# A four-layer graph network on one core: the key sums of the first layer turned, and 1,200 instead of 1,100 edge chunks counted densely

## The chip, the core and the metric

The kernel runs on one NeuronCore of a Trainium2 chip. The core's engines are TensorE (PE in the rows; PEld is its weight load), VectorE (DVE), ScalarE (ACT), GpSimd (POOL) and SyncE (SP, which here only issues DMAs). Each runs its own instruction stream, and they meet at semaphores. The metric is device time in microseconds of one execution; lower is better. SBUF is the on-chip memory of 128 partitions, PSUM holds what TensorE writes, and DRAM tables are reached by DMA.

## The reference

```python
# x (12500, 64); src, dst (400000,), dst sorted; edge_type (400000,) 0 or 1; two edge weights
head = x[src]; rel = relation_emb[edge_type]
score = sigmoid(concat([head, rel]) @ att_w + att_b)
aggr = segment_sum(score * x[dst], src)                 # first layer: sums by src
x = layernorm(x + tanh(aggr @ W0.T + b0))
agg = segment_sum(x[src], dst); deg = segment_sum(1, dst)   # second layer: sums by dst
x = layernorm(x + where(deg > 0, agg, x) @ W1.T + b1)
x = layernorm(x + segment_sum(x[src] * w1, dst))        # third
x = layernorm(x + segment_sum(x[src] * (w2 * w1), dst)) # fourth
```

In the first layer the score depends on the source node and the edge type alone. So the kernel needs, for each pair (node, type), which it calls a key (`2 * src + type`), the plain sum of `x[dst]` over the edges with that key. It multiplies by the score afterwards.

## The kernel before

The 400,000 edges, sorted by `dst`, are 3,125 chunks of 128. A group is 5 chunks (`GC`). Since `dst` is sorted, and denser at low numbers, a chunk of low number touches only 3 to 6 neighbouring nodes (`rows_of`).

**The first layer's main stage** forms the key sums in two ways at once.

*By table*, for the groups from `G00 = C0 // GC` on, `NT0 = 405` of them (`for n in range(NT0)`). DVE (`keys0`) compares each chunk's keys with each other. PE gathers (L1036) and multiplies with `x` (L1053), so that every first edge of a key holds the chunk's whole message for it. ACT copies the message into one of two buffers (`MSGS = 2`, L872) once the scatters that read that buffer have landed. POOL then issues five indirect DMAs that add the 128 messages of each chunk into one of three DRAM tables (L718).

*Densely*, for the first `C0 = 1100` chunks. They are cut into 800 blocks of 1 to 5 chunks. DVE makes a one-hot array for a block (`block_hots0`, L1410), ACT the other factor ("codes", L825 and L830), and PE multiplies the two (`block_sums0`, L1002): this counts how many edges of each key go to each of the block's few nodes. DVE adds the counts into a window of 64 nodes (`block_add0`, L1435). Blocks are listed in windows (`SEGS0`), 29 of them. When the blocks of a window are in, the window is emptied in 25 units (`NU`) of up to 4 tiles of 128: PE turns the counts (`turn`, L1014), ACT copies them to SBUF and clears the window (L844, L849), PE multiplies by the window's rows of `x` (`key_sums`, L1025), and DVE adds the product to `acc` (`key_add`, L1450). There is one set of window counts, so the blocks of the next window start only when all 25 units are through. `xb`, the window's rows of `x`, stands as a block-diagonal 128 x 128: x for type 0 in one corner, x for type 1 in the other.

**The order** is written out ahead by `slots()`: it spreads the dense work over the table groups by costs per block (`0.13*k*d + 0.24*d`) and per unit (2.4). Every engine runs group n of the table work together with the blocks and units of slot n. Before, a slot is worth 7.74 of these cost units.

**The end of the first layer** goes in `NB = 14` batches of 7 node tiles. SP loads a batch of the three tables (L615), POOL adds the three together (L769, L771), DVE adds `acc` (L1528), multiplies by the scores (L1532) and adds the two types (L1536). PE transposes (`turn_sums`, L1074) and multiplies by W0 (`times_w0`, L1082), ACT copies (L883) and takes the tanh (L889), and DVE does the layernorm (L1541 to L1566). Three more layers follow, of other code: the change does not touch them.

Of the kernel before, what the change touches and what calls it, by code (L numbers as in the profile page):

```python
# [17 lines left out]
F32, I32, I16, BF16 = mybir.dt.float32, mybir.dt.int32, mybir.dt.int16, mybir.dt.bfloat16  # L18
# [4 lines left out]
P = 128  # L23
# [8 lines left out]
T = (N + P - 1) // P  # L32
NP = T * P
LAST = N - (T - 1) * P
BT_ = 7
NB = T // BT_
BN = BT_ * P
KEYS = 2 * NP
ROWS = KEYS + P
# [6 lines left out]
NT = (C - CD) // GC  # L46
# [11 lines left out]
BR = 10  # L58
PSD = 4
FZ = 14  # L60
C0 = 1100
G00 = C0 // GC
NT0 = NG - G00
MSGS = 2
# [42 lines left out]
NSEG = len(SEGS) - 1  # L107
SEGS0, SEG_OF0 = segments(NB0, WD, 5)
NS0 = len(SEGS0) - 1
# [67 lines left out]
NU = -(-T // 4)  # L177
# [10 lines left out]
def padded(n):  # L188
    return -(-n // 8) * 8


ND, ND0, NTT = padded(NBLK), padded(NB0), padded(NT)


NCB = CD - C0
# [25 lines left out]
def program(nc, x, src, dst, edge_type_2, edge_weight, edge_weight_n2, rel, att_w, att_b, W0, b0, W1, b1, out):  # L221
    ctx = ExitStack()
    with ctx:
        def sb(name, shape, dt=F32):
            return ctx.enter_context(nc.sbuf_tensor(name, shape, dt))

        def sem(name):
            return ctx.enter_context(nc.semaphore(name))
# [19 lines left out]
        src_i = src_i.bitcast(I32)  # L248
        y = big[:, 0:2 * CQ * P]
        w1_c, w12_c = (big[:, 2 * CQ * P + k * C:2 * CQ * P + (k + 1) * C] for k in range(2))  # L250
        dinfo = sb("dinfo", [1, ND + ND0 + NTT + 64 + 32 + padded(NCB)], I16)

        xs = sb("xs", [P, T * XW])
        acc = sb("acc", [P, NP])


        arena = mem[:, 0:AR]
# [88 lines left out]
        bmin, segb, boff = (arena[0:1, 3125 + k * ND:3125 + k * ND + NBLK] for k in range(3))  # L346
        rows0 = 3125 + 3 * ND
        segb0, boff0 = (arena[0:1, rows0 + k * ND0:rows0 + k * ND0 + NB0] for k in range(2))
        gmin = arena[0:1, rows0 + 2 * ND0:rows0 + 2 * ND0 + NT]
        rows1 = rows0 + 2 * ND0 + NTT  # L350
        sbase, sbase0 = arena[0:1, rows1:rows1 + NSEG], arena[0:1, rows1 + 32:rows1 + 32 + NS0]
        nq_row = stat[0:1, 0:Q]
        assert NSEG <= 32 and NS0 <= 32 and rows1 + 32 + NS0 <= 8455
        STAGED = AR + 2 * CQ * P + 2 * NTAB * BN


        offs_i, offs0_i, cols_i, bases_i, bases0_i, cbase_i = (
            dinfo[:, sum(m[:k]):sum(m[:k + 1])] for m in [(ND, ND0, NTT, 64, 32, padded(NCB))] for k in range(6))
        si = y[:, 0:CD].bitcast(I32)
        badr = r_src  # L360
        kd = dst_l[:, 0:CD]
# [12 lines left out]
        BK = 512  # L374
# [11 lines left out]
        iota_p = ps[:, 7 * BK:7 * BK + DT // 2].bitcast(I16)  # L386
        ps_T = [ps[0:F + 1, 4 * p * BK:4 * p * BK + BN] for p in range(2)]
        ps_B = ps_O = [ps[:, (2 + p) * BK:(2 + p) * BK + BT_ * F] for p in range(2)]
        ps_wt = ps[0:F, 6 * BK:6 * BK + 2 * F]
        ps_dg = ps[:, 6 * BK:6 * BK + T]  # L390

# [20 lines left out]
        z_done, zt_ps = ([sem(f"{n}{l}") for l in range(2)] for n in ("z_done", "zt_ps"))  # L412
        zt_sb, b_done, own_add, deg_ps = (sem(n) for n in ("zt_sb", "b_done", "own_add", "deg_ps"))
        tab_sum, th_done, y_done = sem("tab_sum"), sem("th_done"), sem("y_done")
        tb_in = [sem(f"tb_in{p}") for p in range(2)]
        cmin_done, row_w, row_l, base_done, rows_done = (sem(n) for n in (
            "cmin_done", "row_w", "row_l", "base_done", "rows_done"))
# [549 lines left out]
        def _(pe):  # L967
# [49 lines left out]
            def key_sums(u):  # L1017
                s_, i = u // NU, u % NU
                pe.wait_ge(at_done, u + 1)
                if i == 0:  # L1020
                    pe.wait_ge(xb_in[s_ % 2], (s_ // 2 + 1) * 32)
                if u >= 2:
                    pe.wait_ge(s_add, u - 1)
                for k in range(min(4, T - 4 * i)):
                    last = pe.matmul(ps_s[u % 2][:, k * P:(k + 1) * P], at_sb[u % 2][:, k * P:(k + 1) * P], xb[s_ % 2],  # L1025
                                     start=True, stop=True)
                last.then_inc(s_sum, 1)

            for n in range(NT0):
                kw = rows_of((G00 + n) * GC)  # L1030
# [38 lines left out]
            def turn_sums(b):  # L1069
                pe.wait_ge(z_done[0], b + 1)  # L1070
                if b >= 2:
                    pe.wait_ge(zt_sb, b - 1)
                for k in range(BT_):
                    last = pe.transpose(ps_T[b % 2][0:F, k * P:(k + 1) * P], zb[b % 2][:, k * F:(k + 1) * F], ident[:, :])  # L1074
                last.then_inc(zt_ps[0], 1)

            def times_w0(b):
# [5 lines left out]
                                     start=True, stop=True)  # L1083
                last.then_inc(b_done, 1)

            for b in range(NB + 1):
                if b < NB:
                    turn_sums(b)
                if b:
                    times_w0(b - 1)  # L1090
# [120 lines left out]
        def _(dve):  # L1211
# [312 lines left out]
            def table_sum(b):  # L1524
                v.wait_ge(tab_sum, 2 * (b + 1))
                if b:
                    v.wait_ge(z_done[0], b)
                v.tensor_tensor(tsum, stage[b % 2][:, 0:BN], acc[:, b * BN:(b + 1) * BN], ALU.add).then_inc(sum_done, 1)  # L1528
                v.wait_ge(sum_done, b + 1)
                t4 = tsum.rearrange("p (j t f) -> p j t f", t=2, f=F)  # L1530
                a4 = att.rearrange("p (t j) -> p j t", t=2)[:, b * BT_:(b + 1) * BT_, :]
                v.tensor_tensor(t4, t4, a4.unsqueeze(3).to_broadcast([P, BT_, 2, F]), ALU.mult).then_inc(e0x, 1)  # L1532
                v.wait_ge(e0x, b + 1)
                if b >= 2:
                    v.wait_ge(zt_ps[0], b - 1)
                v.tensor_tensor(zb[b % 2].rearrange("p (j f) -> p j f", f=F), t4[:, :, 0, :], t4[:, :, 1, :],  # L1536
                                ALU.add).then_inc(z_done[0], 1)
# [273 lines left out]
```

## Time and profile before

| | |
|---|---|
| median of 3 runs | 11974.94 us (11965.58 to 11983.21) |
| profiled execution | 11986.64 us |
| its span, first to last instruction | 11984.9 us |
| POOL, DVE, PE, ACT busy, share of the span | 68%, 63%, 73%, 47% |
| first scatter of the first layer | 103.5 us from the start |
| last scatter | 3888.0 us |
| first gather of the second layer | 4044.92 us |

The profile shows one execution. Times in its rows are microseconds from the start of the span; "busy" is time in which an engine works, and the brackets give idle time ahead of an instruction and what ended it. L718 is line 718 of the kernel. A matmul's printed duration includes its latency, so that back-to-back matmuls overlap in the rows; a merged row's second number is the time from the first start to the last end. One f32 matmul of the code stands as two MATMUL instructions, a transpose as one.

### The profile page before, as it was taken

The page shows a single profiled execution, that of the slowest core. Times are in us where ns is not written, and L with a number is a line of the kernel's source. Part 1 is how long each engine was busy: PE and PEld are TensorE (multiplying, and loading weights), DVE is VectorE, ACT ScalarE, POOL GpSimd, SP SyncE. Part 2 cuts the span into 40 slices and gives each one's busy share as a digit, 9 for nine tenths or more (in the row PEclk, how much of TensorE's full clock was granted, in tenths as well). Part 3 has the DMA queues.
Part 4 walks back from the last instruction along what each step waited for, and adds up shares of the span by engine and source line. Part 5 has one row for each costly group of instructions (what it writes and reads, how often), then busy time and mean ns, then how long its engine had stood idle before and what let it go on. Part 6 is the DMA issues. An engine that isn't in the chain of part 4 may idle for free. (4 is left out here: it accounts for less than half of the span.)

```text
span 11984.9 us, 177157 instructions
## 1 busy us (share of the span) xinstructions
PE 8764.2 (73%) x52953; PEld 6104.8 (51%) x52954; DVE 7520.0 (63%) x19055; ACT 5637.8 (47%) x12807; POOL 8164.1 (68%) x7269
## 2 busy tenths in 40 slices
PE   4777777777776455666666788878887788888886
PEld 2555556565564334445445545545445355444455
DVE  7676666666664655544443777666665776666665
ACT  4655554444443344333332566544443665544443
POOL 5888888888888666666666466666666566666665
PEclk7777777777776576777777799999889899889898
DMA  5343334434433311111111111111111111111111
GB/s 145 38 48 38 39 38 39 38 38 39 38 39 38 87 25 25 24 24 25 24 24 24 29 24 25 25 25 24 25 24 26 30 24 25 25 25 25 23 24 29
DMA packets 669272, 405.76 MB, mean 34 GB/s; under 512 B 471754, under 2 KB 581068, under 8 KB 667065
## 3 DMA queue, kind: packets, MB, share of 16 engines
q0 software_dynamic: 460320, 255.76, 17.8%
q1 hardware_dynamic: 204196, 135.29, 4.4%
q8 instruction: 443, 7.26, 0.3%
q10 hardware_dynamic: 3814, 3.37, 0.1%
q14 instruction: 499, 4.09, 0.1%
HBM read 286.44 MB, written 107.44 MB: 33 GB/s over the span
## 5 line engine op out<-in xcount | busy, mean ns | idle before, releaser
L797 POOL DMA_INDIRECT mem<-xt,mem x5175 | 4897.7, 946 | 2886.3 <-issue 1337.2
L1132 PE MATMUL ps<-mem 128*128 128x392 f32 (+5 forms) x6750 | 2914.1, 537 | 1051.8 <-DVE mem L1688 432.1
L718 POOL DMA_INDIRECT table<-mem,idx x2025 | 3149.6, 1555 | 710.3 <-issue 600.8
L1688 DVE TENSOR_TENSOR mem<-mem,ps 128x392 f32 (+3 forms) x3300 | 1917.1, 581 | 1971.6 <-remote 1002.4
L939 ACT ACTIVATE mem<-iota_f,mem 128x128 f32<-128x128 f32 x4200 | 1319.3, 390 | 2635.6 <-remote 1281.9
L1144 PE MATMUL ps<-mem,xs 128*64 128x94 f32 (+1 forms) x17640 | 2064.1, 270 | 387.2 <-issue 370.2
L1144 PEld LDWEIGHTS ps<-mem,xs 128*64 128x64 f32 (+1 forms) x17640 | 1792.1, 155 | 1045.7 <-issue 994.6
L1669 DVE TENSOR_SCALAR mem<-ps,mem 128x392 f32<-128x392 int16 (+5 forms) x4050 | 2175.1, 556 | 0.0
L1132 PEld LDWEIGHTS ps<-mem 128*128 128x128 f32 (+1 forms) x6750 | 1108.5, 185 | 1910.5 <-issue 1303.2
L918 ACT COPY mem<-zero_c 128x658 f32<-128x658 f32 x1260 | 895.8, 732 | 1403.1 <-remote 966.4
L1165 PE MATMUL ps<-mem 128*64 128x64 f32 (+1 forms) x10350 | 1024.4, 243 | 505.5 <-issue 477.3
L1165 PEld LDWEIGHTS ps<-mem 128*64 128x64 f32 (+1 forms) x10350 | 865.1, 155 | 922.1 <-issue 892.5
L1025 PE MATMUL ps<-mem 128*128 128x128 f32 x5684 | 885.5, 313 | 345.8 <-ACT mem L844 325.7
L1002 PE MATMUL ps<-mem 128*128 128x392 bf16 (+2 forms) x2200 | 712.8, 462 | 472.0 <-DVE mem L1435 381.3
L1025 PEld LDWEIGHTS ps<-mem 128*128 128x128 f32 x5684 | 816.0, 223 | 401.6 <-ACT mem L844 370.0
L1450 DVE TENSOR_TENSOR acc<-acc,ps 128x512 f32<-128x512 f32 (+1 forms) x700 | 472.5, 677 | 807.8 <-PE ps L1025 702.4
L1435 DVE TENSOR_TENSOR mem<-mem,ps 128x784 f32 (+2 forms) x800 | 785.3, 982 | 195.0 <-PE ps L1002 85.4
L950 ACT ACTIVATE mem<-mem 128x128 f32<-128x128 f32 x2800 | 879.9, 390 | 18.4
L1703 DVE TENSOR_TENSOR acc<-acc,ps 64x64 f32 (+1 forms) x1035 | 217.1, 210 | 1034.0 <-remote 805.6
L872 ACT COPY mem<-ps 128x320 f32<-128x320 f32 x405 | 172.3, 425 | 1322.2 <-DMA table<-mem,idx 1011.2
L1053 PE MATMUL ps<-mem 64*128 64x64 f32 (+2 forms) x4050 | 713.8, 336 | 82.7 <-ACT mem L857 82.6
L1053 PEld LDWEIGHTS ps<-mem 64*128 64x128 f32 (+2 forms) x4050 | 649.6, 244 | 217.2 <-issue 100.0
(178 smaller groups left out, 7691.6 us busy)
## 6 DMA issues: line engine op xcount, KB each, us to landing
mem<-xt,mem POOLq DMA_INDIRECT x5175
mem<-key_rows SPq DMA_DIRECT2D x405, 160.0 KB
table<-mem,idx POOLq DMA_INDIRECT x2025
table<-mem POOLq DMA_DIRECT2D x3, 6304.0 KB
mem<-table SPq DMA_DIRECT2D x42, 448.0 KB, 5.3
xt<-xs SPq DMA_DIRECT2D x9, 896.0 KB
mem<-in_x_dram SPq DMA_DIRECT2D x403, 16.0 KB
mem<-in_x_dram SPq DMA_DIRECT2D x250, 1.2 KB
```

Source lines behind the costliest of these rows:

```text
L718: pool.indirect_dma_start(out=tables[i % NTAB][:, :], out_offset=bass.IndirectOffsetOnAxis(ap=idx[:, i % (IDXS * GC):i % (IDXS * GC) + 1], ...
L797: pool.indirect_dma_start(out=gbuf[:, o:o + F], out_offset=None, in_=xt[l][:, :], in_offset=bass.IndirectOffsetOnAxis(ap=src_q[q % 2].bitc ...
L918: act.copy(dense[zi // FZ % 2][:, lo * WC:hi * WC], zero_c[:, :].to_broadcast([P, (hi - lo) * WC])).then_inc(cleared[l], 1)
L939: ins = act.activation(lo_d[:, k * P:(k + 1) * P], iota_f[:, 0:P], ACT.Abs, bias=nslo_q[q % 2][:, c + k:c + k + 1])
L950: ins = act.mul(lo_l[:, o + k * P:o + (k + 1) * P], lo_d[:, k * P:(k + 1) * P], wd_q[q % 2][:, c + k:c + k + 1])
L1025: last = pe.matmul(ps_s[u % 2][:, k * P:(k + 1) * P], at_sb[u % 2][:, k * P:(k + 1) * P], xb[s_ % 2], start=True, stop=True)
L1053: last = pe.matmul(ps_m[:, k * F:(k + 1) * F], bts[0:kw, k * P:(k + 1) * P], rhs, start=True, stop=True)
L1132: last = pe.matmul(ps_d[b % PSD][:, 0:w], lo_l[:, r * P:(r + 1) * P], blk_l[:, r * DT:r * DT + w], start=(k == 0), stop=(k == parts - 1))
L1144: last = pe.matmul(ps_f[0:M, :], xs[:, t * XW:t * XW + M], dense[s_ % 2][:, t * WC:(t + 1) * WC], start=(t == 0), stop=(t == T - 1), skip_ ...
L1165: last = pe.matmul(ps_w[n % 2][0:M, :], gbuf[:, o:o + M], ohr[:, q:q + WD], start=(k == 0), stop=(k == GC - 1), skip_group_check=True)
L1669: ins = v.tensor_scalar(blk_l[:, r * DT:r * DT + w], iota_p[:, 0:w], kd_q[q % 2][:, at + k:at + k + 1], None, ALU.is_equal)
L1688: v.tensor_tensor(at, at, new, ALU.add).then_inc(d_add[l], 1)
```

## The change

**Key sums.** The counts, which were the weights of four f32 matmuls of 128 columns, are now streamed as up to 512 columns through one f32 matmul whose weights are the block-diagonal `xb`. Its result is transposed: `acc` holds (type, feature) on the partitions and nodes along the free dimension. So each of the 98 tiles of `acc` must be turned back before the tables are added to it. `turn_back` does this on PE in two parts for each batch, 4 tiles and 3 tiles, through one PSUM bank, and DVE adds the tables in two pieces from there.

**Dense chunks.** `C0` goes from 1100 to 1200. Then `NT0` is 385 instead of 405, there are 900 blocks instead of 800 (the 100 new ones of one chunk and 5 rows each), 35 windows instead of 29, 875 units instead of 725, and 1,925 scatters instead of 2,025. `slots()` spreads the greater dense work over fewer table groups: a slot is worth 9.62 cost units. The rest of the diff finds room for the longer lists.

```diff
+BACK = [(0, 4), (4, BT_)]
-C0 = 1100
+C0 = 1200
...
+        ps_back = ps[:, 6 * BK:7 * BK]
...
         # key_sums
-                for k in range(min(4, T - 4 * i)):
-                    last = pe.matmul(ps_s[u % 2][:, k * P:(k + 1) * P], at_sb[u % 2][:, k * P:(k + 1) * P], xb[s_ % 2],
-                                     start=True, stop=True)
-                last.then_inc(s_sum, 1)
+                w = min(4, T - 4 * i) * P
+                pe.matmul(ps_s[u % 2][:, 0:w], xb[s_ % 2], at_sb[u % 2][:, 0:w], start=True, stop=True).then_inc(s_sum, 1)
...
+            def turn_back(b, half):
+                if b or half:
+                    pe.wait_ge(back_used, 2 * b + half)
+                lo, hi = BACK[half]
+                for k in range(lo, hi):
+                    t = b * BT_ + k
+                    last = pe.transpose(ps_back[:, (k - lo) * P:(k - lo + 1) * P], acc[:, t * P:(t + 1) * P], ident[:, :])
+                last.then_inc(back_ps, 1)
+
+            pe.wait_ge(s_add, NU * NS0)
+            turn_back(0, 0)
             for b in range(NB + 1):
                 if b < NB:
+                    turn_back(b, 1)
+                    if b + 1 < NB:
+                        turn_back(b + 1, 0)
                     turn_sums(b)
                 if b:
                     times_w0(b - 1)
...
         # table_sum
-                v.tensor_tensor(tsum, stage[b % 2][:, 0:BN], acc[:, b * BN:(b + 1) * BN], ALU.add).then_inc(sum_done, 1)
-                v.wait_ge(sum_done, b + 1)
+                for half, (lo, hi) in enumerate(BACK):
+                    v.wait_ge(back_ps, 2 * b + half + 1)
+                    v.tensor_tensor(tsum[:, lo * P:hi * P], stage[b % 2][:, lo * P:hi * P], ps_back[:, 0:(hi - lo) * P],
+                                    ALU.add).then_inc(back_used, 1)
+                v.wait_ge(back_used, 2 * (b + 1))
+                v.sem_inc(sum_done, 1)
```

The order on PE in the stretch where the blocks have three rows (128x294): L1002 is `block_sums0`, L1053 and L1036 the table group's two steps. Before:

```order
L1002 MATMUL ps<-mem 128x294 x14
L1053 MATMUL ps<-mem 128x64 x5
L1036 MATMUL ps<-mem 64x128 x5
L1002 MATMUL ps<-mem 128x294 x12
L1053 MATMUL ps<-mem 128x64 x5
```

and after the change, where these lines are L1006, L1055 and L1038:

```order
L1006 MATMUL ps<-mem 128x294 x16
L1055 MATMUL ps<-mem 128x64 x5
L1038 MATMUL ps<-mem 64x128 x5
L1006 MATMUL ps<-mem 128x294 x18
L1055 MATMUL ps<-mem 128x64 x5
```

A block is two of these matmuls, so 7 blocks stood beside one table group, and 8 or 9 stand there now.

The order on PE while a window is emptied: L1014 are the transposes, L1025 the key sums, 4 and 4 to a unit. Before:

```order
L1053 MATMUL ps<-mem 128x64 x5
L1036 MATMUL ps<-mem 64x128 x5
L1014 MATMUL ps<-ident,mem 128x128 x8
L1025 MATMUL ps<-mem 128x128 x4
L1014 MATMUL ps<-ident,mem 128x128 x4
L1025 MATMUL ps<-mem 128x128 x8
L1053 MATMUL ps<-mem 128x64 x5
```

and after, with L1018 and L1029 for the same:

```order
L1055 MATMUL ps<-mem 128x64 x5
L1038 MATMUL ps<-mem 64x128 x5
L1018 MATMUL ps<-ident,mem 128x128 x8
L1029 MATMUL ps<-mem 128x512
L1018 MATMUL ps<-ident,mem 128x128 x4
L1029 MATMUL ps<-mem 128x512
L1018 MATMUL ps<-ident,mem 128x128 x4
L1029 MATMUL ps<-mem 128x512 x2
L1055 MATMUL ps<-mem 128x64 x5
```

Three units stood between two table groups, and four stand there now; a unit's four products are one.

The order on PE at the end of the layer, where L1074 turns a batch's sums and L1082 multiplies them by W0. Before:

```order
L1074 MATMUL ps<-ident,mem 64x128 x14
L1082 MATMUL ps<-w0T,mem 128x64 x7
L1074 MATMUL ps<-ident,mem 64x128 x7
L1082 MATMUL ps<-w0T,mem 128x64 x7
L1074 MATMUL ps<-ident,mem 64x128 x7
```

and after, where L1094 is `turn_back`, L1076 and L1084 the other two:

```order
L1094 MATMUL ps<-ident,acc 128x128 x11
L1076 MATMUL ps<-ident,mem 64x128 x7
L1094 MATMUL ps<-ident,acc 128x128 x7
L1076 MATMUL ps<-ident,mem 64x128 x7
L1084 MATMUL ps<-w0T,mem 128x64 x7
L1094 MATMUL ps<-ident,acc 128x128 x7
```

The 3 tiles of a batch's second part now stand behind the W0 product of the batch two before it, and 4 tiles of the next batch's first part follow them.

## Rows read from the trace of the kernel before

**Rows 1.** Windows: start:end and length, busy (instructions) by engine, clock, DMA.
```profile
200.00:3800.00 3600.00, 2764.36 (x16446) 2104.51 (x16444) 2374.06 (x7652) 1854.06 (x3502) 3001.24 (x1939) 0.74 0.40 39
1237.00:1265.00 28.00, 26.72 (x229) 24.88 (x228) 18.06 (x65) 16.92 (x33) 23.42 (x16) 1.00 0.39 38
1194.00:1237.00 43.00, 32.86 (x150) 21.50 (x150) 35.82 (x113) 23.53 (x42) 34.44 (x23) 0.53 0.41 39
1237.00:1302.00 65.00, 50.18 (x383) 43.99 (x381) 36.60 (x126) 34.44 (x69) 54.32 (x36) 0.88 0.40 39
3902.00:4038.00 136.00, 64.26 (x294) 58.35 (x294) 109.11 (x105) 34.81 (x53) 85.31 (x43) 0.50 0.55 142
```

**Rows 2.** Waits from 1000 to 3800: who waited for whom, in total, times, longest.
```profile
ACT mem L872 <- DMA table<-mem,idx: 695.6, 164, 9.4
...
PE ps L1002 <- DVE mem L1435: 327.4, 334, 6.0
...
DVE mem L1435 <- PE ps L1002: 58.8, 72, 1.4
...
POOL table L718 <- ACT mem L872: 4.4, 5, 2.1
```

**Rows 3.** Timeline, POOL: start, us, instruction, idle before it.
```profile
1302.48 1.54 POOL L718 DMA_INDIRECT table<-mem,idx  x1 [0.30 <-issue]
```

**Rows 4.** Timeline, ACT's message copies, 1207 to 1296, and POOL where it stood.
```profile
1207.30 0.43 ACT L872 COPY mem<-ps 128x320 f32<-128x320 f32 x1 [4.08 <-DMA table<-mem,idx]
1218.39 0.43 ACT L872 COPY mem<-ps 128x320 f32<-128x320 f32 x1
...
1219.10 1.54 POOL L718 DMA_INDIRECT table<-mem,idx  x1 [2.10 <-ACT mem L872]
...
1231.53 0.43 ACT L872 COPY mem<-ps 128x320 f32<-128x320 f32 x1 [2.48 <-PE ps L1053]
1242.98 0.43 ACT L872 COPY mem<-ps 128x320 f32<-128x320 f32 x1 [1.99 <-PE ps L1053]
1250.67 0.43 ACT L872 COPY mem<-ps 128x320 f32<-128x320 f32 x1 [1.99 <-PE ps L1053]
...
1295.18 0.43 ACT L872 COPY mem<-ps 128x320 f32<-128x320 f32 x1 [7.29 <-DMA table<-mem,idx]
```

**Rows 5.** Timeline, ACT's message copies, 2724 to 2745.
```profile
2724.88 0.43 ACT L872 COPY mem<-ps 128x320 f32<-128x320 f32 x1 [1.41 <-PE ps L1053]
...
2744.04 0.43 ACT L872 COPY mem<-ps 128x320 f32<-128x320 f32 x1 [2.28 <-PE ps L1053]
```

**Rows 6.** Groups by line and form, 200 to 3800, DVE.
```profile
L1435 DVE TENSOR_TENSOR mem<-mem,ps 128x784 f32 x547 | 551.0, 1007 | 136.3 <-PE ps L1002 58.8 <-issue 50.9 <-DVE idx L1345 25.2
...
L1450 DVE TENSOR_TENSOR acc<-acc,ps 128x512 f32<-128x512 f32 x667 | 458.5, 688 | 785.9 <-PE ps L1025 683.6 <-issue 77.5 <-DVE acc L1450 24.8
...
L1435 DVE TENSOR_TENSOR mem<-mem,ps 128x588 f32 x200 | 172.8, 864 | 42.8 <-PE ps L1002 22.3 <-issue 15.1 <-DVE idx L1345 5.4
...
L1410 DVE TENSOR_SCALAR mem<-ps,mem 128x294 bf16<-128x294 int16 x200 | 74.9, 376 | 0.0
```

**Rows 7.** Timeline, PE: a unit's key sums, and a 490-column product of layer four.
```profile
1487.04 1.16 PE L1025 MATMUL ps<-mem 128*128 128x128 f32 x8 [0.24 <-ACT mem L844]
...
11649.25 1.09 PE L1132 MATMUL ps<-mem 128*128 128x490 f32 x2
```

**Rows 8.** Timeline, end of the first layer, DVE and PE.
```profile
3978.24 0.63 DVE L1536 TENSOR_TENSOR mem<-mem 128x448 f32<-128x448 f32 x1
...
3980.42 3.09 PE L1082 MATMUL ps<-w0T,mem 65*128 65x64 f32 x14
...
3981.16 1.08 DVE L1528 TENSOR_TENSOR mem<-mem,acc 128x896 f32<-128x896 f32 x1
```

**Rows 9.** Groups by line and form, 3890 to 4060, DVE.
```profile
L1532 DVE TENSOR_TENSOR mem<-mem,att 128x896 f32<-128x896 f32 x14 | 27.7, 1977 | 0.5
...
L1528 DVE TENSOR_TENSOR mem<-mem,acc 128x896 f32<-128x896 f32 x14 | 18.2, 1302 | 34.1 <-POOL mem L771 34.1
```

## What the change does to the time: the prediction

> **What bounds the kernel now.** I read the page first: no engine is busy for more than 73% of the span, so the stages must be read apart. All that changes lies in the first 4,045 us, and the windows of that stretch are the next view [rows 1]. POOL issued 1,939 scatters in 3,600 us, 1.857 us each. One scatter takes 1.54 us with 0.30 us ahead of it that no engine caused [rows 3], which is 1.84. So the main stage runs at POOL's own pace: 5 x 1.857 = 9.28 us for a table group.
>
> The waits say how near the others are [rows 2]. ACT waited 695.6 us of 2,800 for scatters to land before it could copy the next message; POOL waited for that copy 4.4 us, five times. So the dense side, all that PE, DVE and ACT do, has slack on average. Its stretches differ. How far it is ahead shows in one pair of rows: a copy starts at 1295.18 after 7.29 us of waiting [rows 4], and the group's first scatter is at 1302.48 [rows 3]. About 7 us is the most there can be, since the two message buffers are then full.
> - Blocks of three rows, 7 beside a group: copies at 1207.30 and 1218.39, 11.09 us apart, slower than POOL, and POOL then stood 2.10 us [rows 4]. The clock is 0.53 there [rows 1], but DVE is the one waited for: PE waited 327.4 us for L1435, and L1435 58.8 for PE [rows 2].
> - Blocks of four rows, 5 beside a group: 2724.88 to 2744.04 is two groups, 9.58 us each [rows 5].
> - Units: six took 11.45 us (1231.53 to 1242.98, after a stretch at half clock), four took 7.69 us (to 1250.67) [rows 4]. The clock is 1.00 and PE is busy 26.72 of 28 us [rows 1], so units are PE's.
>
> So a window goes behind in its blocks and catches up in its units.
>
> **The change, part by part.**
>
> *Fewer scatters.* 2,025 - 1,925 = 100, at 1.857 us: -185.7 us, if POOL keeps its pace. Nothing else could take the room on POOL: it does nothing more in this stage.
>
> *Key sums turned.* Six of eight weight loads of a unit go, and eight instructions of 128 columns become two of 512. The columns are the same, and so should be the time: a unit's products take 1.16 us now, first start to last end, and one f32 product of 490 columns in the fourth layer took 1.09 [rows 7]. Scaled to 512 that is 1.14 at most. I take the unit as unchanged; its bounds are -0.1 and +0.1 us. ACT's and DVE's part of a unit has the same shapes.
>
> The Trainium skill, "TensorE: Matmul & The Clock Gate", section "Step-by-step: what each phase is for", says that PE pulls the next weight load ahead beside the matmul in flight. By that rule the six loads that go were free, and the sum stays as it is. If they had stood in PE's way at some 0.1 us each, four units would take 2.4 us less than the 7.69; the row with 1.09 us for one wide product speaks for the rule.
>
> *Denser slots.* A slot holds 9.62 of the planner's units for 7.74, so 1.24 times the blocks or units go beside each group. Per block DVE has 0.864 + 0.376 = 1.24 us at three rows [rows 6], a little less where they overlap: I take 1.2. At four rows the add alone is 1.007 [rows 6], with the one-hot in proportion 1.35.
> - Three rows: 200 blocks, six windows of 33. 8.7 blocks to a group, 11.09 + 1.7 x 1.2 = 13.1 us, 3.8 behind POOL. Over 33 / 8.7 = 3.8 groups that is 14.6; 7 are covered by the lead, 7.6 are stall: 6 x 7.6 = 46 us.
> - Four rows, one chunk each: 14 windows of 25. 6.5 blocks to a group, 9.58 + 1.3 x 1.35 = 11.3, 2.05 behind, 3.85 groups: 7.9, less 7 leaves 0.9: 14 x 0.9 = 13 us.
> - Four rows, several chunks each, six windows at the start: no row at the new density. Between nothing and 4 us a window; I take 10 in all. Five rows, nine windows of few blocks: nothing.
> - Units: 4 beside a group for 3.2, 7.69 us, 1.59 less than POOL, over 6.2 groups: 9.9 us caught up, less 1.1 for the first group, which starts at half clock (11.45 where 7.69 + 2 x 1.33 = 10.35). That is 8.8, enough to be 7 ahead again for the next window. DVE's part, 0.688 us a unit [rows 6], is under PE's.
>
> Sum 69 us, less the 4.4 of before: +65. Bounds: nothing, if blocks go faster when packed, and 150, if each of 29 windows loses 3 us more because the lead is not refilled.
>
> *Turning back.* 14 batches. From 3902 to 4038 DVE is busy 109.11 of 136 us at clock 0.50 [rows 1]; it sets the pace there or nearly. The add itself costs about the same: 0.69 for 4 tiles, by L1450's 0.688, and less for 3, for one of 1.08. New is that the second piece waits for PE. PE's three transposes come after DVE has read the first piece, as both use one bank, and stand behind the W0 product of the batch two before. In [rows 8] the sum of the types starts at 3978.24, PE is in L1082 from 3980.42 to 3983.51, and the table add starts at 3981.16. Its first piece would end near 3981.9; PE comes free at 3983.5 and needs some 0.9 us for three transposes at half clock (my estimate: L1082's 14 instructions in 3.09 us are 0.22 each, and a first one's latency comes on top). DVE waits 2.5 us. Where the layernorm scale of a slice lies between, or PE is idle, about 1. Some comes back: DVE's multiply took 1.977 on average for 1.09 alone, where POOL's adds ran beside it [rows 9], and a DVE that waits meets fewer of them. I take 1.7 a batch, +24 us; bounds 8 (the shuffle of DVE and POOL gives most back) and 45 (3.2 each). The next batch's four transposes lie beside DVE's multiply and add, and are free.
>
> The Trainium skill, "SBUF — State Buffer", section "Who interferes with whom", has a DVE operation with both inputs in SBUF contend with a GpSimd operation that reads SBUF. L1528 took 1.302 on average [rows 9] and 1.08 alone [rows 8], which agrees. With one input in PSUM it would be spared that: some 3 us less over 14 batches, inside the bounds above.
>
> *The start.* The key codes are made over 1,200 columns for 1,100, by ten instructions while POOL waits for its first groups: +1 us.
>
> Sum: -185.7 + 65 + 24 + 1 = -96 us. The profiled execution was 11986.64 us, 12 over the median of the runs; against it that is 11,891, and against the median of 11,974.94, **11,879 us**.
>
> **Rivals.**
> A. *POOL never stands.* ACT's 695.6 us of waiting is room, and the planner's costs may suit. Against it: 11.09 us and 2.10 of standing already at 7 blocks. Then -185.7 + 16 = 11,805. 0.16.
> B. *The gain goes to stalls.* Every window fails to refill the lead, and stalls rise to 150, with 25 for turning back: 11,965. For it: the first group of a window's units took 11.45 us. Against: the next took 7.69. 0.10.
> C. *Slower: PE's clock in the units.* If the units run at a lower clock than 1.00, they catch nothing up, and the dense side is the bound in every window. At full clock a group of four is 7.69; at a mean of 0.85 it is 9.05, and 6.2 x 1.36 = 8.4 us, of which some 6.5 reach the end, come on top in each of 35 windows: 228 - 96 = +132, less what the standing POOL hides: about 12,085. It decides from a mean clock of about 0.90 down. For it: over a whole window's units, 1237 to 1302, the clock was 0.88 [rows 1]. Against: that was with PE idle because ACT waited for POOL; when PE was pushed (1237 to 1265) it was 1.00. 0.12.
> D. That the orientation alone pays: bounded above, it moves no case.
>
> **Numbers.** The forecast has 0.62. Its own range is 11,840 to 11,920. The range that holds 8 of 10 goes down to A, 11,805, and up to B, 11,965; C lies outside. A measurement of this kernel can tell some 0.2%, 24 us, from no change. Faster by more: the forecast, A, and the better part of B: 0.81. Within: 0.06. Slower: C and a rest, 0.13.
>
> **What would show it.** In the trace after: 1,925 scatters at 1.54 and 0.30; the last one near 3,765 (3888 - 186 + 65); POOL waiting for the message copy some 60 to 80 us, most of it between 900 and 1,600 us, in the stretch of 128x294 blocks, and hardly any after 2,500; four units in 7.6 to 7.8 us; f32 products of 512 columns at 1.1 us a pair, start to end; DVE waiting for PE ahead of the second piece of each table add, 1 to 3 us, 14 times; the stretch from last scatter to first gather 20 to 30 us longer than its 157. The forecast is wrong if POOL stands over 120 us or under 20, if four units take over 8.5 us, or if the clock of the units is below 0.9.

## The result, and the profile after

The changed kernel takes 11885.29 us (median of 4 runs, 11878.79 to 11888.68); the kernel before, beside it, 11979.08 (4 runs, 11965.58 to 11994.42). The ratio is 0.9922, 95% interval 0.991 to 0.9934: 94 us faster, where the forecast had 96. The profiled execution took 11878.79 us, with a span of 11877.0 (before: 11986.64 and 11984.9).

All of the gain is in the first layer, and two starts tell how it comes about. The views by line, of the kernel after, for the scatters (L722, L718 before) and for the gathers that open the next stage (L801):

```profile
L722 POOL DMA_INDIRECT table<-mem,idx x1925: 1533/1543/7118, 103.7 to 3775.0; - x193
```

```profile
L801 POOL DMA_INDIRECT mem<-xt,mem x5175: 942/947/1312, 3946.8 to 11822.0; - x200
```

Before, the last scatter started at 3888.0 and the first gather at 4044.92. So the scatters end 113.0 us earlier, and the stretch between the two grew from 156.9 to 171.8 us. At the first gather the change is 98.1 us ahead; from there on nothing was changed, and that part took 7930.2 us in the one profiled execution and 7940.0 in the other. In four further kernels of the experiments, on the same chip, it took 7923.2 to 7931.4 us. So the same code differs by up to 17 us from trace to trace, and small gains are read below from the first layer alone where that is possible.

Windows after: of the main stage, of one group beside nine three-row blocks, and of the end of the layer [rows 1 for before].

```profile
200.00:3700.00 3500.00, 2872.41 (x13060) 1632.85 (x13059) 2592.56 (x7765) 2083.19 (x3894) 2862.14 (x1846) 0.77 0.39 38
1239.70:1252.80 13.10, 8.75 (x35) 4.10 (x34) 11.76 (x32) 7.86 (x14) 8.37 (x6) 0.50 0.34 29
3789.00:3930.00 141.00, 87.20 (x382) 72.81 (x383) 94.69 (x109) 31.04 (x45) 79.39 (x43) 0.50 0.53 136
```

In the first row POOL (the last of the five engines) issues 1,846 scatters in 3,500 us, 1.896 each, where it was 1.857. The second row is the one to remember: for 13.10 us VectorE is busy for 11.76, while PE, at half clock, is busy for 8.75. In the third, VectorE is busy for 67% of the time, where it was 80%: it now waits for PE.

Waits from 1000 to 3800 us, after [rows 2 for before]. ACT waited 695.6 us for scatters before; now that is 322.5, and it waits for PE's messages instead.

```profile
ACT mem L876 <- PE ps L1055: 401.1, 164, 7.0
...
PE ps L1006 <- DVE mem L1451: 348.6, 415, 5.3
...
ACT mem L876 <- DMA table<-mem,idx: 322.5, 85, 9.1
```

POOL's waits for the message copy, after, from 150 to 900, 900 to 1900 (all 200 three-row blocks lie there, with 115 four-row blocks) and 1900 to 3900 us. Before there were 4.4 us in five waits, all in the second stretch.

```profile
POOL table L722 <- ACT mem L876: 21.5, 16, 3.0
...
POOL table L722 <- ACT mem L876: 50.9, 20, 5.0
...
POOL table L722 <- ACT mem L876: 6.6, 5, 2.4
```

Together 79.0 us, 74.6 more than before. 100 scatters less at 1.857 us and 74.6 us of standing make -111.1 for the last scatter's start, where -113.0 was measured. The 79.0 is one trace. Experiment 7 below has the same main stage, on another chip, and its POOL stood 93.4 us and issued its last scatter 9.8 us later: differences of standing of some 14 us are not clear of that spread.

ACT's message copies and one scatter, after, where POOL stands [rows 4 for before]:

```profile
1239.26 0.43 ACT L876 COPY mem<-ps 128x320 f32<-128x320 f32 x1 [1.04 <-PE ps L1055]
1252.24 0.43 ACT L876 COPY mem<-ps 128x320 f32<-128x320 f32 x1
...
1282.83 0.43 ACT L876 COPY mem<-ps 128x320 f32<-128x320 f32 x1 [1.95 <-PE ps L1055]
1290.42 0.43 ACT L876 COPY mem<-ps 128x320 f32<-128x320 f32 x1 [1.95 <-PE ps L1055]
1298.01 0.43 ACT L876 COPY mem<-ps 128x320 f32<-128x320 f32 x1 [1.95 <-PE ps L1055]
```

```profile
1252.94 1.55 POOL L722 DMA_INDIRECT table<-mem,idx  x1 [3.35 <-ACT mem L876]
```

The first two copies are 12.98 us apart, the three behind them 7.59 each: a group beside nine three-row blocks, and groups beside four units. Over the whole run, read from all rows of this kind, eleven groups with nine three-row blocks took 13.8 us on average (this one is the shortest), and seven with eight took 12.4. What fills the 13 us is on VectorE. Its timeline in that group:

```profile
1246.61 0.39 DVE L1426 TENSOR_SCALAR mem<-ps,mem 128x294 bf16<-128x294 int16 x1
1246.92 0.97 DVE L1451 TENSOR_TENSOR mem<-mem,ps 128x588 f32 x1
1247.79 0.38 DVE L1426 TENSOR_SCALAR mem<-ps,mem 128x294 bf16<-128x294 int16 x1
1248.07 0.90 DVE L1451 TENSOR_TENSOR mem<-mem,ps 128x588 f32 x1
1248.85 0.40 DVE L1426 TENSOR_SCALAR mem<-ps,mem 128x294 bf16<-128x294 int16 x1
1250.26 0.77 DVE L1451 TENSOR_TENSOR mem<-mem,ps 128x588 f32 x1 [1.01 <-PE ps L1006]
```

One-hot (L1426) and block add (L1451) follow each other without a gap, about 1.2 us a block, up to the last row: there VectorE waits 1.01 us for PE, once in the group.

### The profile page after: what moved, and what is told of

Its sections match the earlier page's. It is cut to its first block and busy times, and to the rows that moved or that the text cites. A ratio compares the mean times of both kernels' runs of the same rounds, so it can differ in the third digit from the quotient of the medians.

```text
span 11877.0 us, 171360 instructions
## 1 busy us (share of the span) xinstructions
PE 8897.3 (75%) x49605; PEld 5666.5 (48%) x49606; DVE 7726.7 (65%) x19171; ACT 5860.3 (49%) x13187; POOL 8022.3 (68%) x7169
## 5 line engine op out<-in xcount | busy, mean ns | idle before, releaser
L801 POOL DMA_INDIRECT mem<-xt,mem x5175 | 4910.8, 949 | 2864.1 <-issue 1338.3
L722 POOL DMA_INDIRECT table<-mem,idx x1925 | 3000.4, 1559 | 746.4 <-issue 556.7
L1006 PE MATMUL ps<-mem 128*128 128x392 bf16 (+2 forms) x2400 | 786.9, 460 | 520.1 <-DVE mem L1451 414.3
L1451 DVE TENSOR_TENSOR mem<-mem,ps 128x784 f32 (+2 forms) x900 | 902.1, 1002 | 187.8 <-PE ps L1006 83.9
L1029 PE MATMUL ps<-mem 128*128 128x512 f32 (+1 forms) x1750 | 932.3, 634 | 106.6 <-ACT mem L848 82.5
L1466 DVE TENSOR_TENSOR acc<-acc,ps 128x512 f32<-128x512 f32 (+1 forms) x850 | 573.9, 677 | 659.7 <-PE ps L1029 625.9
L1055 PEld LDWEIGHTS ps<-mem 64*128 64x128 f32 (+2 forms) x3850 | 617.9, 244 | 322.8 <-issue 240.7
L1055 PE MATMUL ps<-mem 64*128 64x64 f32 (+2 forms) x3850 | 678.9, 337 | 71.6 <-ACT mem L861 71.6
L829 ACT ACTIVATE mem<-iota,mem 128x256 bf16<-128x256 f32 x1200 | 504.6, 496 | 444.7 <-PE ps L1006 434.3
L1006 PEld LDWEIGHTS ps<-mem 128*128 128x128 bf16 x2400 | 211.5, 111 | 1014.0 <-issue 854.8
```

The lines of the kernel that those rows point to most:

```text
L722: pool.indirect_dma_start(out=tables[i % NTAB][:, :], out_offset=bass.IndirectOffsetOnAxis(ap=idx[:, i % (IDXS * GC):i % (IDXS * GC) + 1], ...
L801: pool.indirect_dma_start(out=gbuf[:, o:o + F], out_offset=None, in_=xt[l][:, :], in_offset=bass.IndirectOffsetOnAxis(ap=src_q[q % 2].bitc ...
L1006: last = pe.matmul(ps_pair[b % 2][:, t * BK:t * BK + w], lo0[:, q:q + P], blk0[:, r * DT:r * DT + w], start=(k == 0), stop=(k == parts - 1 ...
L1029: pe.matmul(ps_s[u % 2][:, 0:w], xb[s_ % 2], at_sb[u % 2][:, 0:w], start=True, stop=True).then_inc(s_sum, 1)
L1055: last = pe.matmul(ps_m[:, k * F:(k + 1) * F], bts[0:kw, k * P:(k + 1) * P], rhs, start=True, stop=True)
L1451: v.tensor_tensor(at, at, new.rearrange("p t (s d) -> p t s d", s=T), ALU.add).then_inc(d0_add, 1)
```

## The experiments

Twelve kernels ran, in three groups of four: experiments 1 to 4; 5 to 7 with e8; 8 with e11 to e13. The second and third group ran on other chips than the first, and there all kernels are some 1,200 us shorter, before too (see the last section). So every time is given against the kernel before of the same group: 11979.43 us (21 runs), 10773.6 (15) and 10767.62 (7). What the change itself gained is 94 us, from the result. "Standing" is POOL's waiting for the message copy in the three stretches used above. Two theories compete from experiment 3 on. The lead theory says that POOL stands where a window falls behind by more than the two buffers hold; deeper buffers would help. The window theory says that a window's blocks and units together take the dense side longer than POOL needs for that window's groups; no buffer helps there, only less dense work, or more groups for that window. In the forecast of experiment 3 they are Theory 1 and the rival.

**1. The dense counting without the turn.** `C0 = 1200`, all else as before:

```
-C0 = 1100
+C0 = 1200
```

> The dense part of the change alone: 1,200 chunks, key sums as four products of 128 columns, no turning back. Theory 1 (the orientation costs only the turning back, and a unit's time is set by its columns): POOL stands as long as in the changed kernel, 76 us give or take 15, the stretch from last scatter to first gather goes back from 172 to about 157 us, and the time is 11,870 us, 15 under the changed kernel. Theory 2 (the wide product pays inside the units, by the weight loads that go): units are slower, POOL stands 110 us or more, and the time is 11,890 to 11,920 us.

Measured: 11869.58 us, ratio 0.9909 (0.9894 to 0.9924), 109.9 us under before. So the dense counting alone brings the whole gain, and a little more. POOL stood 102.7 us in it, 24 more than in the changed kernel, and its last scatter started at 3787.5, 12.5 us later; but from there to the first gather it took 154.9 us against 171.8. Time and stretch are those of theory 1, the standing lies outside its 61 to 91 and short of theory 2's 110. The turned units are a little cheaper: the median of the groups beside four units is 7.69 us here and 7.59 in the changed kernel. By my estimate that is 0.025 us a unit, 22 us over 875 units, which is of the size of the 24 us; but against the 93.4 us of experiment 7, with turned units too, only 9 are left, so how much standing the turn saves isn't settled.

**2. The turn without the dense counting** (the changed kernel with `C0 = 1100`).

> The orientation alone, with 1,100 dense chunks. Theory 1: 2,025 scatters at POOL's pace as before, 15 us more at the layer's end: 11,994 us, slower than before by 0.1%. Theory 2: the same or faster than before, 11,970 to 11,980 us, with POOL's standing of 7 us gone.

Measured: 11996.31 us, 1.0013 (1.0004 to 1.0022), 16.9 us over before, as theory 1 had it. The last scatter is at 3892.0 (before 3888.0) and the first gather at 4064.0 (4044.92): 15.1 of the 19.1 us lie in between. While POOL sets the pace (it stood 5.4 us here, 4.4 before), cheaper units give nothing, and the turning back is paid in full.

**3 and 4. A third message buffer**, once on the changed kernel and once on the one before:

```
-MSGS = 2
+MSGS = 3
...
-        msg = arena[:, 5365:5365 + MSGS * GC * F]
+        msg = [arena[:, 5365:5365 + GC * F], arena[:, 5365 + GC * F:5365 + 2 * GC * F],
+               sb("msg", [P, GC * F])[:, :]]
...
```

> The changed kernel with three message buffers instead of two, so that the dense side may be some 16 us ahead of POOL instead of 7. Theory 1 (each window falls behind in its blocks by more than the lead, and catches up in its units): POOL's standing falls from 76 us to under 20, and the time to about 11,825 us. Rival (in the windows of three-row blocks the dense side is slower than POOL over the whole window, so that no lead is ever built up): it stays at 60 or more, and the time at 11,870 to 11,885 us.

> The kernel before with three message buffers. Both theories: POOL stood 7 us there, so the third buffer has at most that to give: 11,972 us, the same as before within the noise. If it gains more than 20 us, the buffer does something that neither theory has.

Measured: 11872.19 us, 0.991 (0.9895 to 0.9926), and 11977.72 us, 0.9999 (0.999 to 1.0008). By the medians the third buffer is worth 107.2 - 94 = 13 us on the changed kernel, but at the first gather only 7.6 us (3939.2 for 3946.8), and POOL stood 77.2 us in all, for 79.0; on the kernel before it is worth nothing, as both theories had it. The lead theory had under 20 us of standing and 11,825 us, its rival 60 or more and 11,870 to 11,885. POOL's waits in e3 from 900 to 1900, one row for each place that a message lies in:

```profile
POOL table L722 <- ACT mem L875: 34.0, 16, 5.0
POOL table L722 <- ACT msg L875: 19.2, 8, 5.0
```

That is 53.2 us, where it was 50.9. More room for a lead does not shorten the standing where it is longest. My theory, that the size of the lead decides, fell here. The window theory stands: in these windows the dense side needs longer than POOL over the window as a whole, so no lead builds up that a buffer could hold.

**5 and 6. Fewer and more chunks**: the changed kernel with `C0 = 1150` and with `C0 = 1250`.

> The changed kernel with 50 chunks fewer counted densely (C0 = 1150). Both theories take 92.9 us for 50 scatters more. Window theory: POOL stands because whole stretches of the dense side (three-row windows: mean step 9.9 to 10.2 us) run slower than POOL's 9.25 us per group; with ten groups more for the same windows most of them fall under that pace, and the standing falls from 76 us to about 20: 11,922 us (11,905 to 11,935). Lead theory (the prediction's): each group of eight or nine three-row blocks takes 12 to 14 us and outruns a lead of 7 us now and then; such groups stay nearly as many, the standing falls to about 40: 11,942 us or more.

> The changed kernel with 50 chunks more counted densely (C0 = 1250); 92.9 us of scatters go. Window theory: the 50 blocks of five rows (about 1.5 us each) and their share of the product cost the dense side more than POOL saves, and ten groups fewer are left to hide them behind: nearly every window is slower than 9.25 us per group, the standing rises from 76 us to 250 to 300: about 11,990 us (11,940 to 12,030), slower than with 1200. Lead theory: the standing rises with the number of long groups only, to about 110: 11,826 us.

Measured: 10722.5 us, 0.9953 (0.9939 to 0.9967), 51.1 under before, and 10753.97 us, 0.9983 (0.9974 to 0.9992), 19.6 under before. POOL's waits in the three stretches, with 1250:

```profile
POOL table L722 <- ACT mem L876: 75.6, 32, 6.9
...
POOL table L722 <- ACT mem L876: 122.8, 39, 6.5
...
POOL table L722 <- ACT mem L876: 87.1, 49, 5.3
```

285.5 us, in every stretch, against 33.9 with 1150 and 79.0 with 1200. Per 50 scatters, 92.9 us go; the standing takes back 45 of them from 1150 to 1200, and 206 from 1200 to 1250. So 1200 lies where the dense side is about to become the bound everywhere. With 1250 both numbers lie inside the window theory's ranges, and the lead theory is off by 134 us. With 1150 the time is inside the window theory's range and the gain 14 us more than the lead theory allows; the standing of 33.9 us is nearer to the lead theory's 40 than to the other's 20.

**7. The W0 product later.** On PE the product of batch b-1 is issued behind the second piece of batch b+1:

```
             turn_back(0, 0)
+            turn_back(0, 1)
             for b in range(NB + 1):
-                if b < NB:
-                    turn_back(b, 1)
-                    if b + 1 < NB:
-                        turn_back(b + 1, 0)
+                if b + 1 < NB:
+                    turn_back(b + 1, 0)
+                if b < NB:
                     turn_sums(b)
+                early = b - 4 in [hi // BT_ - 1 for _, hi in SLICES]
+                if b and early:
+                    times_w0(b - 1)
+                if b + 1 < NB:
+                    turn_back(b + 1, 1)
-                if b:
+                if b and not early:
                     times_w0(b - 1)
```

> The changed kernel; at the layer's end the weight product of batch b-1 is issued after the second piece of the next batch is turned back, instead of ahead of it. If the 2.34 us waits of VectorE ahead of the second piece (27.6 us in 14 waits) are on the path that sets the end of the layer, they fall to about 1.0 us and the last scatter to first gather goes from 172 to about 160 us: 11,875 us. Rival: GpSimd's two table additions a batch (2.16 and 2.28 us) or the product itself take the wait's place: no change, 11,885.

Measured: 10667.77 us, 0.9901 (0.9886 to 0.9916), 105.8 under before, and 163.6 us from last scatter (3784.8) to first gather (3948.4), for 171.8. This stretch hardly varies from trace to trace: in six kernels with the turn as made it is 171.8 to 173.8 us, in both with the later product (this and e11) 163.6 and 163.7, in six with the old orientation 154.8 to 156.9. So the 8 us are shown, though the two kernels ran on different chips. It is not the 12 us that the forecast had, and in these two traces it is hidden by the longer standing ahead of it: the first gather starts at 3948.4 here and at 3946.8 in the changed kernel. The same wait, in the changed kernel and here:

```profile
DVE mem L1546 <- PE ps L1094: 27.6, 14, 2.9
```

```profile
DVE mem L1551 <- PE ps L1094: 14.6, 14, 1.6
```

13.0 us of waiting go, 8.2 arrive. The rest went into longer operations of DVE. The scores (L1552, here L1557) and the sum of the types (L1556, here L1561), in the changed kernel:

```profile
L1552 DVE TENSOR_TENSOR mem<-mem,att 128x896 f32<-128x896 f32 x14 | 26.2, 1873 | 2.0
L1556 DVE TENSOR_TENSOR mem<-mem 128x448 f32<-128x448 f32 x14 | 17.5, 1251 | 0.5
```

and with the later product:

```profile
L1561 DVE TENSOR_TENSOR mem<-mem 128x448 f32<-128x448 f32 x14 | 26.4, 1883 | 0.5
L1557 DVE TENSOR_TENSOR mem<-mem,att 128x896 f32<-128x896 f32 x14 | 21.9, 1567 | 2.0
```

These two together take 48.3 us instead of 43.7: VectorE, no longer waiting, runs into more of POOL's adds. One such meeting in this kernel:

```profile
3835.37 2.81 POOL L775 TENSOR_TENSOR mem<-mem 128x896 f32<-128x896 f32 x1
3836.28 2.39 DVE L1561 TENSOR_TENSOR mem<-mem 128x448 f32<-128x448 f32 x1
```

Alone the sum of the types takes 0.63 us. That agrees with what the Trainium skill, "SBUF — State Buffer", section "Who interferes with whom", says: a VectorE operation with both inputs in SBUF contends with a GpSimd operation that reads SBUF. It is why a wait taken off VectorE here is worth less than its length.

**8. Half the add.** In three-row blocks VectorE adds 294 of 588 elements; the kernel leaves out the other half, so its sums are incomplete, and it serves the timing alone. Its edit, in part:

```
+                if rows == 3:
+                    at, new = at[:, 0, :, :], new[:, 0, :, :]
...
```

> The changed kernel, in which VectorE adds only the first half (294 of 588 elements a partition) of each three-row block's counts to the window: the second half is left out. In one step of nine such blocks VectorE was busy for 11.76 of 13.10 us. If VectorE is what makes these steps long, 200 blocks get some 0.4 us cheaper each, a step of eight or nine falls from 12.3 to 13.9 us to about 9 to 10.5, and the 40 us that POOL stands in the three-row windows (of 76 in all) go: gain on before grows from 94 to about 130 us. Rival: the steps are bound by TensorE at half clock or by the chain over ScalarE's message copy: the steps shorten by under 1 us, POOL still stands 60 us or more, and the gain stays near 100 us.

Measured: 10625.38 us, 0.9869 (0.9852 to 0.9885), 142.2 under before. The add, from 900 to 1900, in the changed kernel and here, and POOL's waits in that stretch here:

```profile
L1451 DVE TENSOR_TENSOR mem<-mem,ps 128x588 f32 x200 | 172.3, 862 | 41.8 <-PE ps L1006 21.3 <-issue 16.9 <-DVE idx L1361 3.6
```

```profile
L1454 DVE TENSOR_TENSOR mem<-mem,ps 128x294 f32 x200 | 100.6, 503 | 59.9 <-PE ps L1006 32.9 <-issue 19.6 <-DVE idx L1361 3.6
```

```profile
POOL table L722 <- ACT mem L876: 8.1, 8, 2.5
```

50.9 us become 8.1, and nothing moves in the other stretches (22.4 and 7.9, for 21.5 and 6.6). Nothing of PE's or ACT's work was touched, and PE's clock stayed (0.73 and 0.74 from 900 to 1900; 0.50 in one of these groups of either kernel). This shows that VectorE's work on the three-row blocks is what POOL stands for, and that shortening it is enough at PE's half clock. The steps of nine blocks got shorter by 2 us only (13.8 to 11.8 on average, from ACT's copies, where the forecast had 9 to 10.5), less than the 3.2 us taken out of them. Two things come close behind by the rows: VectorE's waits for PE's products in this stretch rose from 30.3 to 48.4 us, and the message copies wait longer for scatters (33.8 us for 20.1 from 996 to 1611), as they do where POOL sets the pace.

**9 to 12. Versions.** Now the knobs that the window theory names: the three-row blocks entered at more than their old cost, so that the planner gives those windows more groups, and 1175 chunks. The third buffer is in all four. e8, e12 and e13 have the old orientation, e11 the new one with the later product of experiment 7. The planner's line, in e8, e11 and e12 (in e13 the factor is 1.18, and 1.07 for the blocks of the first 300 chunks):

```
-    [0.13 * k * d + 0.24 * d for (_, k), d in zip(BLOCKS[:NB0], ROWS_OF)]
+    [(0.13 * k * d + 0.24 * d) * (1.15 if d == 3 else 1) for (_, k), d in zip(BLOCKS[:NB0], ROWS_OF)]
```

> Old orientation of the product (as e1_dense_only), C0 = 1175, three message buffers, and three-row blocks entered at 1.15 of their cost where the counting is dealt out to the groups, so that the full windows get more groups. Window theory: 46.4 us of scatters come back against e1_dense_only (11,870), but all windows fall under POOL's pace and its standing goes from 94 to under 15 us: about 11,830 us (11,815 to 11,850). Lead theory: a third buffer was worth nothing and long groups stay: standing 60 us or more, about 11,885.

> New orientation with the later weight product (e6), C0 = 1175, three message buffers, three-row blocks entered at 1.15: as e8_best, which stood 124.5 us under before, but turned. If the orientation gives back in the counting what it costs at the layer's end (12 us less of standing against 8 us more at the end, after e6), it is level with e8_best: 115 to 130 us under before. Rival: with POOL's standing already down to 25 us there is nothing left for the cheaper units to give, and only the turning back is left to pay: about 115 us under before.

> e8_best with C0 = 1200 instead of 1175: 25 scatters fewer (46.4 us). Window theory: ten groups in fewer are left for 25 more five-row blocks; the dense side has no spare on the whole, so dealing the counting out evenly moves standing from the three-row windows to later ones and saves little: standing 60 to 95 us, 105 to 115 us under before, worse than e8_best. Rival (dealing out was what helped, not fewer chunks): standing stays near 25 us, about 170 us under before.

> e8_best with the costs of the counting raised further: three-row blocks at 1.18, blocks of the first 300 chunks at 1.07. Where POOL stood most in e8_best (9.0 us in window 2, 4.8 in window 0 with the start) it should stand less, at most 15 us gained: 125 to 140 us under before. Rival: the leads of later windows are used up and standing only moves there: same as e8_best within 5 us.

| kernel | us | ratio (95%) | under before | standing | last scatter | first gather |
|---|---|---|---|---|---|---|
| e8 old, 1175 | 10649.09 | 0.9884 (0.9869 to 0.9899) | 124.5 | 27.8 | 3767.5 | 3923.7 |
| e11 turned, 1175 | 10643.64 | 0.9888 (0.9872 to 0.9905) | 124.0 | 14.3 | 3759.3 | 3923.0 |
| e12 old, 1200 | 10635.92 | 0.9879 (0.9863 to 0.9896) | 131.7 | 73.7 | 3762.3 | 3917.1 |
| e13 old, 1175, more even | 10634.13 | 0.9877 (0.986 to 0.9893) | 133.5 | 11.1 | 3756.2 | 3912.2 |

e8 fell 5 us short of its range's slow end: its standing was 28 us, not under 15. In e13 it is 11.1 us, inside the forecast for the time, and some 40 us beyond the change as made; its lead of 1.8 us on e12 is not clear of noise, the runs of the two overlap. e12 refutes both of its forecasts: its standing is that of the window theory (73.7, in 60 to 95), the time is 17 us better than it said, for the same dense counting undealt (e1_dense_only) stood 102.7 us and was 109.9 us under before, so dealing out and a third buffer did save something at 1200 too. In the stretch from 900 to 1900 the standing went from 64.2 us in e1 to 30.6 in e12, which the third buffer alone did not do (53.2 for 50.9), so there it was the dealing out. The two were not tried apart with the old orientation. e11 and e8 are level, as the first forecast for e11 had it: in their two traces the turned kernel is 8 us ahead at the last scatter and loses 7.5 behind it. The 7.5 repeats in the stretches above; the 8 is within what the same main stage differed by between two chips (9.8 us).

## Why the prediction was right

The mechanism held: POOL's pace sets the main stage, it stands some 75 us longer, most of that in the windows of three-row blocks, and the end of the layer grows by the turning back. Each term of the sum came within 10 us. That the total came within 2 us is luck: standing was 9.6 us more than forecast and turning back 9.1 us less, and the two cancel. By the traces' own measure the gain is 98.1 us at the first gather and 108 us at the end.

- *Fewer scatters*, -185.7: 1,925 are there, at 1.54 and mostly 0.30 us. Right.
- *Stalls*, +65: measured +74.6. By window, from POOL's rows: the six with the bulk of the three-row blocks have 45.2 us for 46, the six ahead of them 23.7 for 10, all behind them 10.2 for 13. The early windows are the term that was mis-sized: there was no row for them, and "between nothing and 4 us a window" was a guess that came out at its upper end.
- *How a stall comes about.* The prediction let a window lose 14.6 us in its blocks, cover 7 of them with the lead, and catch up 8.8 in its units, "enough to be 7 ahead again". By the same numbers a window loses 14.6 and gains 8.8, so it is 5.8 us too long whatever the lead; that only two buffers are there adds no more than 1.8 to that. I read this as a matter of buffers when I planned e3, and was wrong there: with a third buffer the stretch still has 53.2 us, for 50.9. The numbers had been right, the reading of them was not.
- *What a step costs.* 13.1 us for 8.7 blocks: the 18 groups with eight or nine such blocks took 13.3 on average, and 1.2 us a block is what VectorE's rows show. That VectorE is the one waited for was read from [rows 2]; experiment 8 bears it out.
- *Units unchanged*: 7.59 us for four, for 7.69 before (forecast 7.6 to 7.8), at a granted clock of 1.00 from 1275 to 1298. Over the units of a whole window it is 0.91 to 0.98 in all windows but the short last one, so above the 0.9 that the forecast named. Key sums of a pair in one row of PE:

```profile
1496.62 1.13 PE L1029 MATMUL ps<-mem 128*128 128x512 f32 x2 [0.24 <-issue]
```

  1.13 us for 1.16 [rows 7]: six weight loads fewer gave 0.03 us a unit, inside the bounds of 0.1. The rule of the Trainium skill ("TensorE: Matmul & The Clock Gate", "Step-by-step: what each phase is for") that the next load is pulled ahead beside the matmul in flight agrees with that.
- *Turning back*, +24: +14.9, so the stretch grew by less than the 20 to 30 us that were to show the forecast right. The waits are of the two kinds that were said, seven of 2.34 us, four of about 1 and three from 1.65 to 2.87, 27.6 in all: after the first piece, PE is in the W0 product, and the second piece follows 2.34 us late.

```profile
3832.68 3.08 PE L1084 MATMUL ps<-w0T,mem 65*128 65x64 f32 x14
3833.42 0.68 DVE L1546 TENSOR_TENSOR mem<-mem,ps 128x512 f32<-128x512 f32 x1
...
3835.55 0.85 PE L1094 MATMUL ps<-ident,acc 128*128 128x128 f32 x3
...
3836.44 0.56 DVE L1546 TENSOR_TENSOR mem<-mem,ps 128x384 f32<-128x384 f32 x1 [2.34 <-PE ps L1094]
```

  What comes back was sized well. The sum of the types fell from 1.501 to 1.251 us and the scores from 1.977 [rows 9] to 1.873, 5.0 us over 14 batches, and the 34.1 us that L1528 had waited for POOL [rows 9] are 27.3 of idle time ahead of the first piece now, 6.8 less. With 0.9 us less for the add these are the 12.7 between 27.6 and 14.9. That is 0.9 us a batch, and I had allowed 0.8, from 2.5 to 1.7. What was too large is the wait: I had in effect taken 2.5 in every batch, 35 us in all, though I had said that some would be about 1. The add itself was to be some 3 us shorter with one input in PSUM. Its pieces did stay short beside POOL's adds (0.55 to 0.69 us, all 28, where the old add ran up to 2.75), but two pieces take 1.24 us where one took 1.08 alone, and the whole is 17.3 us for 18.2.
- *The start*, +1: the first scatter is at 103.7 for 103.5. The rest of the ledger, -98.1 less the four terms as measured, is about -2 us and isn't assigned.

Of the rivals, A needed a dense side with room everywhere; the 79 us refute it. B needed twice the standing. C needed slower units, and 7.59 us a group at full clock, and a time 94 us shorter, rule it out. With 1250 chunks the gain does go to stalls as B has it, though with 285.5 us of standing, not 150. D, that the turn alone pays, fails: it costs 17 us in experiment 2. How much it costs beside 1200 chunks isn't settled: 4.4 us by the first gathers of the two traces (3946.8 and 3942.4), 16 by the medians; 11 us of that lie in code that is the same in both.

## What to carry to other kernels

When two sides of a pipeline are matched by hand, sum each window for both sides before asking how deep the buffers are: a window that is too long as a whole is not helped by a buffer. It is helped by less work, or by dealing the work out in proportion to measured costs, so that it stands beside more of the other side's work; together with a third buffer that was worth some 22 us here at 1,200 chunks, and the reorientation nothing. And try the two halves of a combined change apart: one half carried all of the gain here, and the other cost 4 to 16 us beside it.

## What the runs showed of the hardware that was not expected

The same program differs by 10% between chips, and only in a part of it. The kernel before took 11979 us on one chip and 10774 and 10768 on two others. The first layer is nearly the same: the changed kernel on the first chip and e6 on another have the same code up to the last scatter, which starts at 3775.0 in the one and at 3784.8 in the other. Behind the first layer, where all of these kernels have the same code, the gathers run from 3942.4 to 11810.2 us in e1 on the first chip and from 3948.4 to 10613.9 in e6. What the gathers waited for, in e1:

```profile
  issue: 1334.1, 4377
  remote: 1010.9, 572
  PE ps L1178: 483.6, 223
```

and in e6:

```profile
  issue: 1564.6, 5133
  PE ps L1186: 46.3, 39
```

The waits that the profile puts down to "remote" are gone, on every engine, and the mean granted clock of the whole span is 0.844 for 0.809. What is remote there isn't named by the profile, and no run looked for it. Absolute times do not carry over from chip to chip. Whether differences do was not tried with two kernels on the same two chips; what speaks for it is the end of the first layer, whose length by orientation repeats on all three (experiment 7).

Second, half as many elements do not halve an add of VectorE. On average 588 took 862 ns and 294 took 503. The averages mix quick and slow ones: read from all rows, the quickest took 0.74 us for 588 and 0.44 for 294, so about 0.14 us of each is fixed, beside 1.02 ns an element. The quickest adds of 784 and 980 elements, 0.94 and 1.16 us, lie on the same line. What makes half of the 588s 0.88 us or more isn't settled.
